# Two transformer layers on one core: ScalarE takes the normalisations, and the second layer's projections move into the first feed-forward and the first scores

## What is computed

```python
x = x + ln(attn0(ln(x)))      # latent attention: down-projections, two inner norms, up-projections, rotary
x = x + ln(ffn0(ln(x)))       # silu(x Wg sg) * (x Wu su) then Wd sd, int8 weights, inner size 1024
x = x + ln(attn1(ln(x)))      # plain qkv attention
x = x + ln(ffn1(ln(x)))
# attn: 16 heads of 16 channels, causal, softmax over all keys
```

## Time and profile before

| | us |
|---|---|
| median of 3 runs | 1278.7 (1278.65 to 1279.92) |
| profiled execution | 1275.28 |
| its span | 1273.5 |
| first projections and set-up | to about 86 |
| attention, layer 0 | 86 to about 504 |
| output projection, layer 0 | 504 to 534.5 |
| FFN, layer 0 | 534.5 to 645 |
| projections, layer 1 | 645 to 708 |
| attention, layer 1 | 708 to about 1125 |
| output projection and FFN, layer 1 | to 1273.5 |

### The profile page before, as it was taken

One profiled execution on the slowest core, in us unless ns is written; L12 is line 12 of the kernel. 1 busy time (PEld: TensorE's weight loads), 2 busy tenths in 40 slices (PEclk: granted clock), 3 DMA queues, 4 the chain that ended last, 5 costly groups with the idle time before them and its releaser, 6 DMA issues.

```text
span 1273.5 us, 35512 instructions
## 1 busy us (share of the span) xinstructions
PE 1164.4 (91%) x14872; PEld 586.6 (46%) x14872; DVE 1049.9 (82%) x2746; ACT 720.6 (57%) x919; POOL 334.7 (26%) x561
## 2 busy tenths in 40 slices
PE   5769999999999998799978789999999999987996
PEld 4432344544444543566645224455444445454664
DVE  7759999999999862878863899999999988558776
ACT  2441377767677886234342407777767778843332
POOL 2321211122111133433442212111231112424433
PEclk9976699999999999899999659999999999997998
DMA  5354000211100000000026320021120000000000
GB/s 173 121 160 109 25 15 15 64 28 37 43 3 2 3 4 3 18 16 1 1 77 190 85 87 15 15 56 28 30 58 4 3 3 3 4 1 2 17 18 33
DMA packets 31600, 49.95 MB, mean 39 GB/s; under 512 B 7245, under 2 KB 24143, under 8 KB 31431
## 3 DMA queue, kind: packets, MB, share of 16 engines
q1 hardware_dynamic: 25376, 41.95, 11.9%
q0 software_dynamic: 5488, 5.34, 1.4%
q10 hardware_dynamic: 576, 0.39, 0.1%
HBM read 32.56 MB, written 14.68 MB: 37 GB/s over the span
## 4 chain that ended last, share of the span: by engine, by line
PE 68%; DVE 19%; DMA 4%; ACT 3%; POOL 3%; issue 2%; SPq 1%; ACTq 0%; POOLq 0%; DVEq 0%
PE ps L887 65%; DVE m_tile L780 6%; DVE ps L782 3%; DMA k_parts<-parts 2%; DVE region_p L640 1%; DVE stats L627 1%; ACT region_p L569 1%; DMA q_parts<-parts 1%; PE ps L1034 1%; POOL q_stack L455 1%; DVE region_p L838 1%; PE ps L882 1%; DVE rem L681 1%; POOL parts L423 1%; DVE region_p L754 1%
## 5 line engine op out<-in xcount | busy, mean ns | idle before, releaser
L569 ACT ACTIVATE region_p<-ps 128x1024 f32<-128x1024 f32 (+3 forms) x640 | 541.4, 894 | 246.9 <-PE ps L887 243.4
L780 DVE TENSOR_REDUCE m_tile<-ps 128x1 f32<-128x512 f32 x768 | 501.3, 685 | 28.0 <-PE ps L887 22.5
L887 PE MATMUL ps<-k_stack,q_stack 96*32 96x512 bf16 (+3 forms) x5120 | 435.2, 375 | 21.4 <-DVE v_all L688 7.6
L887 PE MATMUL ps<-q_stack,k_stack 99*32 99x512 bf16 (+3 forms) x5120 | 350.5, 352 | 3.6 <-ACT region_p L569 2.2
L887 PE MATMUL ps<-region_p,v_all 128*17 128x512 f32 (+3 forms) x2560 | 292.8, 531 | 5.0 <-POOL region_p L460 4.8
L782 DVE CUSTOM_DVE_ANT_0 ps<-ps,causal 128x128 f32<-128x128 f32 (+3 forms) x512 | 248.7, 497 | 27.8 <-PE ps L887 26.3
L887 PEld LDWEIGHTS ps<-k_stack,q_stack 96*32 96x32 bf16 x5120 | 144.0, 96 | 256.5 <-DVE m_tile L780 104.0
L887 PEld LDWEIGHTS ps<-q_stack,k_stack 99*32 99x32 bf16 x5120 | 140.3, 98 | 153.3 <-issue 56.7
L460 POOL TENSOR_SCALAR_AFFINE_SELECT region_p<-region_p 128x512 f32<-128x512 f32 x128 | 81.1, 635 | 275.3 <-ACT region_p L569 269.7
L887 PE MATMUL ps<-region_a,w_ffn 128*128 128x512 f16 x512 | 125.8, 392 | 6.1 <-DVE region_a L672 5.2
L603 ACT ACTIVATE k_stack<-ps,cols 128x512 f32<-128x512 f32 x64 | 44.0, 688 | 129.9 <-PE ps L887 125.2
(11 more groups left out here) (93 smaller groups left out, 895.6 us busy)
## 6 DMA issues: line engine op xcount, KB each, us to landing
k_parts<-parts SPq DMA_DIRECT2D x16, 384.0 KB, 7.9
q_parts<-parts SPq DMA_DIRECT2D x16, 384.0 KB, 8.7
q_stack<-q_parts SPq DMA_DIRECT2D x32, 192.0 KB
k_stack<-k_parts SPq DMA_DIRECT2D x32, 192.0 KB
q_stack<-q_parts SPq DMA_DIRECT2D x32, 128.0 KB
k_stack<-k_parts SPq DMA_DIRECT2D x32, 128.0 KB
X<-in_x SPq DMA_DIRECT2D x4, 512.0 KB, 6.6
q_stack<-q_parts SPq DMA_DIRECT2D x32, 64.0 KB
```

The costliest lines, as they stand in the source:

```text
L569: nc.scalar.activation(probs[:, o.j % SLOTS, 2 * o.hp:2 * o.hp + 2, o.off:CH], psT[:, o.k % 2, :, o.off:CH], ACT.Exp, scale=SCALE).then_in ...
L780: nc.vector.tensor_reduce(maximum, scores, AX.X, ALU.max).then_inc(s.ring_free, 1)
L887: return pe.matmul(o, a, b, start=first, stop=last)
```

## The change

1. All norms but turn 0 go to ACT: DVE makes `rstd` and a new `nbias` = -mean * rstd for four tiles, and ACT writes Identity(scale * in + bias), scale and bias being columns.
2. In layer 0 z of a chunk stands directly after its down products (`DVE_BEFORE`, `ACT_BEFORE`).
3. Of layer 1, chunks 0 to 2 (12 units, 6 value pairs, 6 transpose pairs) are threaded through the first FFN, with PSUM banks 6 and 7 in turn; the transposed input is a chunk buffer in the third part of `region_p`. Value pairs 4 and 5 come after the last down product. The last chunk's transposes, four units and two value pairs stand at entries 3 to 16 of layer 1's attention order.
4. SP loads the stacks of group 0 as the chunks come; those of group 1 wait, in both layers, for the first T of step 2.
5. ACT's order in the output projection now has norms between its moves; adds on POOL in the FFN go together at i = 3.

```diff
+    STEP2_T = min(o.k for o in ORDER if o.kind == "T" and o.n == 2)
+        nbias = sb("nbias", [P, NT, 2], F32)
+        x_chunk = region_p[:, NT * C:NT * C + 2 * KC * CH].rearrange("p (b k t) -> p b k t", b=2, k=KC)
...
-            [("qk", m, c) for c in range(NCH) for m in (0, 2)] + [("qk", m, c) for c in range(NCH) for m in (1, 3)],
+            [("qk", m, c) for c in range(NCH) for m in (0, 2, 1, 3)],
...
-        DVE_BEFORE = {0: [("down", 0), ("down", 1), ("z", 0)], 1: [("down", 2), ("c", 0), ("z", 1)],
-                      3: [("down", 3)], 4: [("c", 1), ("z", 2)], 7: [("c", 2), ("z", 3)], 10: [("c", 3)]}
-        ACT_BEFORE = {0: [("sqrt", 0), ("sqrt", 1)], 1: [("c", 0), ("sqrt", 2)], 3: [("sqrt", 3)], 4: [("c", 1)],
-                      7: [("c", 2)], 10: [("c", 3)]}
+        DVE_BEFORE = {0: [("down", 0), ("z", 0), ("down", 1), ("z", 1)], 1: [("down", 2), ("c", 0), ("z", 2)],
+                      3: [("down", 3), ("z", 3)], 4: [("c", 1)], 7: [("c", 2)], 10: [("c", 3)]}
+        ACT_BEFORE = {0: [("sqrt", 0), ("z", 0), ("sqrt", 1), ("z", 1)], 1: [("c", 0), ("sqrt", 2), ("z", 2)],
+                      3: [("sqrt", 3), ("z", 3)], 4: [("c", 1)], 7: [("c", 2)], 10: [("c", 3)]}
...
+        def early_jobs(u):
+            jobs = []
+            for d in range(NCH - 1):
+                i = u - NI * (d + 1)
+                late = 1 if d < NCH - 2 else 0
+                jobs += [(job, d) for job, at in (("branch", 2), ("stats", 4), ("norm", 4 + late), ("x", 5 + late),
+                                                  ("pair0", 6 + late), ("pair1", 7 + late), ("rest", 8 + late)) if at == i]
+            return jobs
...
+        X_AT, UNITS_AT, VALUES_AT, FIRST_T = 3, {8: 12, 10: 13, 12: 14, 14: 15}, 16, min(
+            n for n, o in enumerate(ORDER) if o.kind == "T")
+        REM_AT, VALUES_SB_AT, LOW_AT = {10: 12, 12: 13, 14: 14, 16: 15}, 20, {15: (12, 13), 16: (14, 15)}
...
-                sp.wait_ge(s.t_filled, L * T_N + 1)
+                sp.wait_ge(s.t_filled, L * T_N + STEP2_T + 1)
...
+            def normalize_branch(k, b):
+                act.wait_ge(turn[k].rstd_done, 2 * (b + 1))
+                for i in range(TPC * b, TPC * (b + 1)):
+                    nc.scalar.activation(A[:, i, :], A[:, i, :], ACT.Identity, scale=rstd[:, i, 0:1],
+                                         bias=nbias[:, i, 0:1]).then_inc(turn[k].normed, 1)
...
-                for u in range(4):
+                for u in range(3):
                     o_move(u)
                 sqrt_branch(k1, 0)
+                o_move(3)
+                normalize_branch(k1, 0)
                 o_move(4)
+                sqrt_branch(k1, 1)
                 o_move(5)
-                sqrt_branch(k1, 1)
+                normalize_branch(k1, 1)
                 o_move(6)
                 o_move(7)
+                sqrt_residual(k1, 0)
                 sqrt_branch(k1, 2)
-                sqrt_residual(k1, 0)
+                normalize_residual(k1, 0)
+                normalize_branch(k1, 2)
                 sqrt_branch(k1, 3)
                 move_transposed(k1, 0)
+                normalize_branch(k1, 3)
...
+            def inverse(tn_done, bs, w, at):
+                nc.vector.reciprocal(rstd[:, bs, w], std[:, bs, w]).then_inc(tn_done, 1)
+                dve.wait_ge(tn_done, 2 * at + 1)
+                nc.vector.scalar_tensor_tensor(nbias[:, bs, w], mv[:, bs, w, 0], -1.0, rstd[:, bs, w], ALU.mult,
+                                               ALU.mult).then_inc(tn_done, 1)
...
+                    side(0, "v", 4)
+                    side(0, "v", 5)
+                    pe.wait_ge(f.evac, NT)
+                    pe.wait_ge(p.v_sb, 6)
```

More of the change, by code:

```diff
@@ new lines, in side_jobs @@
+        def side_jobs(L, u):
+            c, i = divmod(u, NI)
+            jobs = [("x16", 2 * c + 2), ("x16", 2 * c + 3)] if u < NCH * NI and i == XHAT_AT[c] + 2 else []
+            for job, d in early_jobs(u) if L == 0 else []:
+                if job == "x":
+                    jobs += [("x", 2 * d), ("x", 2 * d + 1)]
+                if job in ("pair0", "pair1"):
+                    first = 4 * d + 2 * (job == "pair1")
+                    jobs += [("unit", first), ("unit", first + 1)]
+                if job == "rest":
+                    jobs += [("v", 2 * d), ("v", 2 * d + 1)]
+            return jobs
@@ new lines, in build_program, with side_bank, side_release, unit_bank @@
+        UF = NCH * NI
+        SIDE = [[("x16", 0), ("x16", 1)] + [j for u in range(UF + 1) for j in side_jobs(L, u)] for L in range(2)]
+        def side_bank(L, kind, n):
+            return 6 + SIDE[L].index((kind, n)) % 2
+        def side_release(L, kind, n):
+            return {"x16": (turn[1 + 2 * L].moved_v, n + 1), "x": (turn[2].moved_a, n + 1),
+                    "unit": (proj[1].rem, n + 1), "v": (proj[1].v_sb, n + 1)}[kind]
+        def unit_bank(L, u):
+            if L == 1:
+                return side_bank(0, "unit", u) if u < EARLY else (u + 2) % 4
+            return u % 4
@@ L354, in _ @@
                     sp.dma_start(unit_dram(L, u), parts[:, u % PB, :, :]).then_inc(parts_stored[L][u % PB], 16)
[L355 to L358, removed]
+                    c = chunk_ready(L, u)
+                    if c is not None:
+                        parts_complete(chunk_units(L, c))
+                        load_stacks(0, c)
                 parts_complete(NU)
@@ L495, in sqrt_residual, with normalize_residual @@
                                      bias=eps[:]).then_inc(turn[k].std2, 1)
+            def normalize_branch(k, b):
[3 more added lines that the diff above has]
+                                         bias=nbias[:, i, 0:1]).then_inc(turn[k].normed, 1)
+            def normalize_residual(k, b):
+                act.wait_ge(turn[k].rstd2, 2 * (b + 1))
+                for i in range(TPC * b, TPC * (b + 1)):
+                    nc.scalar.activation(A[:, i, :], X[:, i, :], ACT.Identity, scale=rstd[:, i, 1:2],
+                                         bias=nbias[:, i, 1:2]).then_inc(turn[k].xhat, 1)
             def move_transposed(k, b):
@@ L549, in chunk_scalar @@
                         nc.scalar.activation(std[:, bs, :], mv[:, bs, :, 1], ACT.Sqrt, bias=eps[:]).then_inc(p.std, 1)
+                    elif what == "z":
+                        act.wait_ge(p.rstd, 2 * (c + 1))
+                        for i in range(TPC * c, TPC * (c + 1)):
+                            for w, cs in ((0, slice(0, DQ)), (1, slice(DQ, DQ + DKV))):
+                                nc.scalar.activation(c_down[:, i, cs], c_down[:, i, cs], ACT.Identity,
+                                                     scale=rstd[:, i, w:w + 1], bias=nbias[:, i, w:w + 1]
+                                                     ).then_inc(p.z, 1)
                     else:
@@ L599, in _ @@
                     c, i = divmod(u, NI)
+                    if i == 3 and c > 0:
+                        normalize_branch(k2, c - 1)
+                    if i == XHAT_AT[c] + 1:
+                        normalize_residual(k1, c + 1)
+                    for job, d in early_jobs(u) if L == 0 else []:
+                        if job == "x":
+                            normalize_residual(2, d)
                     act.wait_ge(f.gu_ps, u + 1)
@@ L938, in _ @@
                 p = proj[L]
[L939 to L941 removed]
                 if L == 0:
+                    for b in range(NCH):
+                        transpose_batch(0, b)
+                    pe.wait_ge(w_in[0], 16 * 7)
                     pe.wait_ge(turn[0].moved_a, NT // 2)
```

280 lines of the change are left out of this document (176 added, 104 removed).

## The result

The changed kernel takes 1348.0 us (median of four runs, 1342.9 to 1349.8), beside 1278.7 us for the kernel before on the same chip: a ratio of 1.0535 with a 95% interval of 1.0505 to 1.0564. It is slower, by 69 us; forecast were 33 us and at most 51. The profiled execution took 1348.22 us, its span 1346.5, against the 1273.5 of before: the trace has 73.0 us to explain.

The account below looks back on a forecast made before the run. TensorE was taken to bound the kernel (68% of the chain). First projections +9, stalls 2 x 18.5, moved projections -9 and output projections -4 sum to +33: 1308.3 us profiled, 1311.7 against the median; range 1281 to 1330.

Parts of the forecast that it names:

- Stacks of head group 1: Attention, both layers: late-released loads take 33 us against 15.5 of cover, stalling PE 17 us, plus 1.5 for the clock.
- the reckoning in the prediction: Head group 1's stack loads confined to two DMA engines: 37 us of load, stall 21 or 22, total 1322; chance 0.12.
- Output projections: Both layers' output projections: DVE sheds normalisations to ACT, so the FFN starts 2 us earlier each, -4 for both.
- Moved projections: Layer 1's projections put into the first FFN: FFN +29.0, transition to entry 16 -38.3, in all about -9 us.
- The sign that I gave for it: Changed trace: first score of layer two within 7 us of the last FFN product.
- ACT's order in the FFN, I cost it at nothing: First FFN: ACT's some 40 us of added work costs nothing, covered by longer PE iterations and PE being two ahead.
- Rival 3: FFN: ACT's order holds PE back in some 6 iterations by 1.5 us, +9 more, 1321 us; chance 0.08.
- First projections, +9: Layer 0's first projections: z on ACT delays unit 0's remainder 3 us and unit 4's store to about 61.5, +9 us.

Follow-up runs that it names:

- e1: The changed kernel with the loads of head group 1 released by the first T again in both layers; ratio 1.0244 to the kernel before.
- e2: The kernel before with only the late release of head group 1's loads (first T of step 2) added; ratio 1.0337.
- e8: The changed kernel with early release of head group 1, layer 0's z on DVE in the old order, and FFN-loop tiles on DVE; 1267.92 us, ratio 0.9919.
- e7: The changed kernel with all normalised tiles inside both FFN loops on DVE; 1320.98 us, ratio 1.0333.
- e6: The changed kernel with ACT's normalised tiles in the FFN loop moved from ahead of the Silu to right behind it; ratio 1.0389.
- e10: The kernel of e8 with z on DVE but in the changed kernel's order, directly behind its own down chunk; ratio 0.9971.
- e11: The kernel of e8 with z on ACT but at the places of the kernel before; ratio 1.0004.
- e9: The kernel of e8 with layer 1's chunk 3 stack loads issued only after step 0's rows of maxima have landed; ratio 0.9914.
- e13: The kernel of e9 with layer 1's head group 1 loads released by the landing of step 1's rows of maxima; ratio 0.9929.
- e14: The kernel of e13 with the same release of head group 1 in layer 0 too; ratio 0.9953.
- e5: The changed kernel with the normalisation bias made by four one-column tensor_scalar instructions instead of one scalar_tensor_tensor of four; ratio 1.0536.

## Why the prediction was wrong in size

- **Stacks of head group 1: right.** Stalls of 17.2 and 16.9 us, forecast 17. The clock behind them costs more than the 1.5 us put there: e1 and e2 give 19.4 to 20.3 a layer, 20 in place of 18.5, so 3 us of the 36 that were missing. The Trainium skill, "DMA: Bandwidth & Descriptors", rules for kernel authors, would by the reckoning in the prediction have given 21 or 22 us of stall; the trace has 17.
- **Output projections: right.** -2.5 us each, forecast -2; over all runs with that code C and H are 1.2 to 2.9 us under before.
- **Moved projections: right once ACT's order is taken out.** e8 has -9.5, forecast -9.3; entry 16 comes 32.5 us after the FFN's last product in the kernel after (727.4 to 759.9), forecast 32.8. The sign that I gave for it failed: the first score comes 11.7 us after the last product, not within 7, as it waits for the rows of ones; the way to entry 16 does not go over it.
- **"ACT's order in the FFN, I cost it at nothing": this step failed,** and it is the larger miss. The cover that I named, PE being two iterations ahead and longer iterations, was reckoned on busy time (39 us and 40 more in 139). What counts is what stands ahead of the next Silu: a square root's table load, a wait for DVE's reciprocal and bias behind DVE's own queue, four tiles of 2.08 us and the table load back. Stage D loses 19.2 us by it (159.4 against 140.2 in e7) and I 8.1: 27 us. Rival 3 had the mechanism at +9. The Trainium skill, "ScalarE: Activation LUTs", what ACT_TABLE_LOAD costs, has 2.66 us for a switch with its drain; the rows of after have 1.283 us and almost no idle time, in 13 + 10 + 6 + 2 loads (those ahead of the first DMA apart). The cost lay in the order and not in the switch: e6 and e7 have the same 31 table loads, and FFN 1 loses nothing in either. In FFN 0 the order explains 11 of the 19 us (e6); the other 8 go only when the tiles leave ACT (e7).
- **First projections, +9: the term was mis-sized,** it is +17.2. I let DVE wait for ACT's z and followed unit 0's remainder, 3 us later. The rows show three things more. z(0) starts at 30.59 us, not 27.4, and z(1) at 34.98, not 31.8: both 3.2 late, by the later start and the slower first products above, which stand ahead of any z. PE then waits 3.8 us at a time and its clock falls, so the down products take 3.21 us and not 1.61; this I had at nothing. And z takes 3.04 us, not 2.9. So the lateness against my reckoning grows: z(2) ends at 49.15 for 43.8, z(3) at 61.25 for 54.4, unit 4's store is issued at 69.35 for 61.5. Of the 8 us missing, 3.2 are there at the first z and 4.7 come after it. Order and engine cost 7.9 and 11.6 alone (e10, e11), the slower first products included.
- **Layer 1's attention, not in the sum at all: +4 us** without the stall (G in e8). Here the small DMAs with the rows of the maxima stand behind chunk 3's loads, as the loads now follow the first scores and don't precede them. e9, e13 and e14 show that moving loads moves this wait and does not remove it. The kernel before escapes it in layer 1: its last DMA of rows of step 0, issued at 720.7 us, lands in 1.9 us, the 24 loads run from 724.7 to the tail's end at 760, and the rows of step 1, from 761.6, land in 1.6 to 1.7. The loads just fit between two steps. That these landings are all of the 4 us is not shown: e9 took the first away and gained nothing.

Sum: to the forecast 33 come 3 for the clock behind the stalls, 8 for A (3 of them ahead of any z), 27 for ACT's order and 4 for G, and off go 1 for C and H and 0.5 for FFN 1, which without ACT's order is that much shorter than before: 73.5 against the measured 73.0.

## What to carry to other kernels

Work taken off a busy engine must be placed by what stands behind it in the new engine's own order, not by that engine's share of busy time: in the second FFN one normalisation ahead of a Silu cost 2.5 us of TensorE, the same behind it nothing (e6). When a trigger of a bulk load is moved, compare two lengths, trigger to use and issue to landing; here 16 us stood against 33, and that one line cost some 40 of the 69 us. A change made of parts is worth measuring by parts: the parts with the losses undone, this one is 0.8% faster than the kernel it began from.

## What was not expected of the hardware

- VectorE's scalar_tensor_tensor on four columns takes 0.17 us alone and 1.02 us when GpSimd's subtraction of 128x512 starts just ahead of it (1287.10 and 1287.14 us), and ends with it; so in all nine such meetings of the kernel after. Four tensor_scalars on one column took 0.58 in either case (e5).
- PE's granted clock is at 0.50 after waits of 3.95 and 3.75 us in the first projections (windows above), where the kernel before, with waits of 1.57 and 1.91 us, is at full clock; the eight products behind such a wait take 1.6 us longer.
- The first 9 to 13 matmuls of this kernel's projections can run at half their rate (0.35 for 0.18 us) while the granted clock reads 1.00 (after, e2, e10, e11, against before and e8).
- Most DMAs with rows of maxima land 1.6 to 1.7 us after their issue. With stack loads of another queue issued before them the last of a step takes 4.17 us (e9), 5.22 (e13) and 5.94 (e8).
